# Attention probabilities and head outputs transposed by DMA instead of by TensorE, in a fused attention and mixture-of-experts kernel

## What is computed

```python
q = rms_norm((x @ wq).reshape(B, L, 16, 128), q_norm_w)
k = rms_norm((x @ wk).reshape(B, L, 4, 128), k_norm_w)          # then rope on q and k
k_ctx = rms_norm((ctx @ wk_ctx).reshape(B, T, 4, 128), k_norm_w)
scores = jnp.einsum('blhd,bmhd->bhlm', q, k_full) * scale + mask
probs = jax.nn.softmax(scores, axis=-1)
out = jnp.einsum('bhlm,bmhd->blhd', probs, v_full)
x = x + out.reshape(B, L, 16 * 128) @ wo
```

## Time and profile before

| | before |
|---|---|
| median of 3 runs | 376.57 us |
| the profiled execution's own run | 377.97 us |
| its span, first to last instruction | 376.3 us |
| PE busy | 343.7 us, 91% |
| VectorE busy | 325.6 us, 87% |
| ScalarE busy | 271.2 us, 72% |
| GpSimd busy | 165.8 us, 44% |
| mean granted clock of TensorE | 0.977 |
| moved by DMA | 13.49 MB |

### The profile page before, as it was taken

One profiled execution on the slowest core, in us unless ns is written; L12 is line 12 of the kernel. 1 busy time (PEld: TensorE's weight loads), 2 busy tenths in 40 slices (PEclk: granted clock), 3 DMA queues, 4 the chain that ended last, 5 costly groups with the idle time before them and its releaser, 6 DMA issues.

```text
span 376.3 us, 7781 instructions
## 1 busy us (share of the span) xinstructions
PE 343.7 (91%) x2471; PEld 237.3 (63%) x2476; DVE 325.6 (87%) x625; ACT 271.2 (72%) x913; POOL 165.8 (44%) x242
## 2 busy tenths in 40 slices
PE   6697798799999999999999999999999999998994
PEld 5373555376567665866685577567666778674572
DVE  1668999998999899899989998999899897759653
ACT  3557879676986797699759876986797567167562
POOL 3356565652754275427344443644174300334330
PEclk9788989999999999999999999999999999989999
DMA  5967000000030003000000000000000000000011
GB/s 179 379 212 223 17 0 2 1 2 14 3 111 0 14 0 111 14 1 0 0 14 0 0 0 14 0 0 0 0 0 1 2 0 2 2 0 3 22 35 57
DMA packets 11603, 13.49 MB, mean 36 GB/s; under 512 B 824, under 2 KB 9024, under 8 KB 11584
## 3 DMA queue, kind: packets, MB, share of 16 engines
q1 hardware_dynamic: 11584, 13.25, 11.0%
HBM read 12.20 MB, written 1.05 MB: 35 GB/s over the span
## 4 chain that ended last, share of the span: by engine, by line
PE 40%; DVE 24%; ACT 17%; issue 10%; POOL 4%; DMA 2%; SPq 1%; DVEq 1%; ACTq 0%; POOLq 0%
PE proj L1324 10%; ACT probs L524 8%; PE pt_ps L1300 5%; DVE probs L953 5%; PE proj L1157 4%; PE turn L1246 3%; DVE nmax L941 3%; DVE pT_lo L879 3%; PE o_ps L1310 3%; POOL q_rot L744 3%; PE sc_ps L1267 2%; ACT pT_hi L435 2%; DMA wq<-in_L_xattn_wq_dram 2%; ACT q_junk L468 2%; DVE q_t L870 2%
## 5 line engine op out<-in xcount | busy, mean ns | idle before, releaser
L524 ACT ACTIVATE probs<-sc_ps,nbias,q_r 128x256 f32<-128x256 f32 x128 | 70.8, 574 | 2.8 <-DVE nbias L945 2.8
L744 POOL TENSOR_TENSOR q_rot<-q_t 128x512 f32<-128x512 f32 x32 | 41.4, 1295 | 42.8 <-DVE q_t L872 42.0
L953 DVE TENSOR_SCALAR probs<-probs,rden 128x256 f32<-128x256 f32 x128 | 51.2, 461 | 1.1
L1157 PE MATMUL proj<-wq_hi,xT 128*128 128x512 f16 x128 | 40.1, 396 | 2.9 <-DVE wq_lo L863 2.9
L435 ACT ACTIVATE pT_hi<-pt_ps 128x512 f16<-128x512 f32 x64 | 34.8, 597 | 10.9 <-PE pt_ps L1300 10.9
L468 ACT ACTIVATE q_junk<-proj 128x128 bf16<-128x128 f32 x128 | 34.0, 295 | 11.7 <-DVE q_t L872 11.7
L879 DVE SCALAR_TENSOR_TENSOR pT_lo<-pt_ps,pT_hi 128x512 f16<-128x512 f32 x64 | 41.0, 682 | 0.6 <-ACT pT_hi L435 0.6
L941 DVE TENSOR_REDUCE nmax<-sc_ps 128x4 f32<-128x1024 f32 x32 | 38.9, 1214 | 1.5 <-PE sc_ps L1289 1.5
L831 POOL TENSOR_TENSOR wq<-xn_all,weight 128x512 bf16<-128x512 f32 x16 | 17.1, 1074 | 44.1 <-DVE weight L1098 23.4
L1324 PE MATMUL proj<-wo_hi,oT_hi 128*128 128x256 f16 x128 | 34.9, 273 | 0.0
L1324 PE MATMUL proj<-wo_lo,oT_hi 128*128 128x256 f16 x128 | 34.9, 273 | 0.0
(11 more groups left out here) (216 smaller groups left out, 920.7 us busy)
## 6 DMA issues: line engine op xcount, KB each, us to landing
wq<-in_L_xattn_wq_dram SPq DMA_DIRECT2D x4, 512.0 KB, 9.1
w<-in_L_ffn_w_dram SPq DMA_DIRECT2D x2, 1024.0 KB, 10.5
wq<-in_L_xattn_wo_dram SPq DMA_DIRECT2D x1, 2048.0 KB, 8.2
ctx_b<-in_ctx_dram SPq DMA_DIRECT2D x8, 128.0 KB, 2.1
out_dram<-x_all SPq DMA_DIRECT2D x4, 256.0 KB, 2.2
x_all<-in_x_dram SPq DMA_DIRECT2D x1, 896.0 KB, 12.3
wkc<-in_L_xattn_wk_ctx_dram SPq DMA_DIRECT2D x1, 512.0 KB, 4.2
wk<-in_L_xattn_wk_dram SPq DMA_DIRECT2D x1, 512.0 KB, 5.1
```

The source lines that it names most:

```text
L524: last = nc.scalar.activation(probs[:, h, :], sc_ps[:, h, :], ACT.Exp, bias=nbias[:, h:h + 1], scale=q_r[:, g, h:h + 1], accum_out=den[:, ...
L744: nc.gpsimd.tensor_tensor(q_rot[:], q_t1[:], q_t2[:], ALU.add).then_inc(q_added, 1)
L953: last = nc.vector.tensor_scalar(probs[:, h, :], probs[:, h, :], rden[:, h:h + 1], None, ALU.mult)
L1157: last = nc.tensor.matmul(bank[:], xT[:, a, c, :], w[:, c, cols], start=(n == 0), stop=(n == 3 * DC - 1))
```

## The change

The probabilities are no longer divided by their sum before the product with V, and TensorE no longer turns them. ScalarE rounds the undivided probabilities to f16 in SBUF (`p_round`, 128x1024), VectorE makes the rest (`p_rest`), and SyncE issues two transposing DMAs of 128x1024 f16 (256 KB each) into `pT_hi` and `pT_lo`, which have two slots. `p_hi` and `p_lo` have one slot: `p_round` and `p_rest` of a group wait until both DMAs of the group before have landed.

`mix` now has the turned probabilities as its stationary side and V as its moving side: per head 6 products of 128 columns, 24 in a group in place of 6 of 512. Its result has the tokens on the partitions. A group later VectorE multiplies it by the reciprocal sums (`o_scale`, 128x512 from PSUM), ScalarE rounds it (`o_round`), GpSimd makes the rest (`o_rest`), and two transposing DMAs of 128x512 f16 (128 KB each) bring `oT_hi` and `oT_lo`. `out_proj` is cut into four quarters (`out_part`), one in each group of the next row, summed in a bank of its own, `out_ps`; the residual and `second_norm` move to g=3.

Besides: `k_add` moves from VectorE to GpSimd. `kc` has a bank of its own (`kc_ps`) and stands after `k` and `q` on TensorE. On ScalarE `kc_copy` and `k_copy` stand after `p_round`, no longer between exponentials; `kc_scale` stands after `q_squares`. On GpSimd `kc_roots` stands after `q_add` and `k_roots`. wo is loaded in four pieces, w3 and w2 in four each. `xn2T` shares its memory with `w1_32`, and `ahead` and `tied` with `probs`. The sync engine's program is written out for all 32 groups. In the tail the order is adapted: quarters of `out_part` between the turns of weights, the router cut in two around `xn_copy(2)` and the last `o_scale`.

The core of the diff:

```diff
@@ sync
+            def turn_probs(b, g):
+                u = G * b + g
+                slot = u % 2
+                if u >= 2:
+                    sp.wait_ge(pv_done, u - 1)
+                for src, dst, split in ((p_hi, pT_hi, p_high), (p_lo, pT_lo, p_low)):
+                    sp.wait_ge(split, u + 1)
+                    sp.dma_start_transpose(dst[:, slot].rearrange("p h a t -> p (h a) t"),
+                                           src[:].rearrange("p h k -> p (h k)")).then_inc(d_pT[slot], 16)
+
+            def turn_out(b, g):
+                u = G * b + g
+                if b:
+                    sp.wait_ge(wo_part, u - G + 1)
+                for src, dst, split in ((o_hi, oT_hi, o_high), (o_lo, oT_lo, o_low)):
+                    sp.wait_ge(split, u + 1)
+                    sp.dma_start_transpose(dst[:, g, :].rearrange("p (h t) -> p h t", h=R),
+                                           src[:, g % 2, :]).then_inc(d_oT[g % 2], 16)
...
@@ scalar, row
-                    if g or not first:
-                        p_copy(u - 1)
-                    exps(b, g, (kc_copy, k_copy) if g == 3 and not last else ())
+                    exps(b, g)
                     if g == 1 and not first and not last:
                         ln_high(b + 1)
+                    p_round(b, g)
+                    if g == 3 and not last:
+                        kc_copy(b + 1)
+                        k_copy(b + 1)
+                    if g >= 2:
+                        o_round(b, g - 2)
+                    elif not first:
+                        o_round(b - 1, g + 2)
                     if g == 2 and not last:
+                        k_squares(b + 1)
                         kc_squares(b + 1)
                     if ahead_of(b, g, 2, last):
                         q_squares(*ahead_of(b, g, 2, last))
+                    if g == 2 and not last:
+                        kc_scale(b + 1)
...
@@ gpsimd, row
                     if g == 1 and not last:
                         ln_low(b + 1)
+                    if g == 3 and not last:
+                        q_roots(b + 1, 0)
+                    if g == 2 and not last:
+                        k_add(b + 1)
+                    if ahead_of(b, g, 2, last):
                         q_add(*ahead_of(b, g, 2, last))
                     if g == 2 and not last:
                         k_roots(b + 1)
+                        kc_roots(b + 1)
                         k_scale(b + 1)
+                    if g >= 2:
+                        o_rest(b, g - 2)
+                    elif not first:
+                        o_rest(b - 1, g + 2)
+                    if ahead_of(b, g, 2, last) and g != 2:
+                        q_roots(*ahead_of(b, g, 2, last))
+                    if g == 0 and not last:
+                        ln_root(b + 1)
+                    if g == 3 and not first:
+                        l2_root(b - 1)
...
@@ vector, row
-                    if g or not first:
-                        p_low(u - 1)
-                    if g == 2 and not first:
-                        second_norm(b - 1)
+                    if g >= 2:
+                        o_scale(b, g - 2)
+                    elif not first:
+                        o_scale(b - 1, g + 2)
+                    if g == 2 and not last:
+                        k_turn(b + 1)
...
-                    normalise(b, g)
+                    inv_den(b, g)
...
+                    p_rest(b, g)
+                    if g == 0:
+                        vc_low(b)
+                        v_low(b)
...
+                    if g == 3 and not last:
+                        kc_low(b + 1)
+                        k_low(b + 1)
...
+                    if g == 3 and not first:
+                        residual(b - 1)
+                        second_norm(b - 1)
...
@@ tensor
+            def mix(b, g):
+
+                u = G * b + g
+                seen(pe, o_scaled, u)
+                cols = slice(g * P, (g + 1) * P)
+                pe.wait_ge(*landed(d_pT, b, g))
                 for a in range(2):
                     for h in range(R):
+                        for i, (p, v) in enumerate(((pT_hi, v_hi), (pT_hi, v_lo), (pT_lo, v_hi))):
+                            last = nc.tensor.matmul(o_ps[:, h * P:(h + 1) * P], p[:, g % 2, h, a, :], v[:, a, cols],
...
@@ tensor, row
-                    if g or not first:
-                        turn_probs(b, g)
+                    if g == 2 and not last:
+                        k(b + 1)
...
                     if g == 1:
-                        if not first:
-                            out_proj(b - 1)
                         if not last:
                             turn_inputs(b + 1)
                         pe.wait_ge(vc_ready, b + 1)
...
+                    if not first:
+                        out_part(b - 1, g)
                     if g:
-                        mix(u - 1, g - 1)
+                        mix(b, g - 1)
```

353 lines of the change are left out of this document (175 added, 178 removed).

## The result

The changed kernel took 420.93 us, the median of 4 runs (419.65 to 421.62), against 376.86 for the kernel before (376.12 to 378.42, 4 runs): a ratio of 1.1159, 95% interval 1.1113 to 1.1205. The forecast was 400 with a range of 374 to 435. The sign, and the waits that make a steady row, came as foretold; the size was half of what happened, 23 us of 43, and the tail went otherwise than I had it.

The account below looks back on a forecast made before the run. TensorE, 91% busy, bounded the kernel before; afterwards waits between engines would: six rows of +3.2, clock 4, row 0 +3, last row -3.7, tail +0.5, 23 us more, for 400 us, range 374 to 435.

Parts of the forecast that it names:

- TensorE's lighter work is off the path: Steady rows: TensorE's work falls by 3.1 us to about 31, but waits between engines set the row.
- Stretch g=1: Scores of g=1 to scores of g=2: 9.7 us against 11.8, a gain of 2.1, with TensorE idle over 3 us.
- Stretch g=2 and 3: Scores of g=2 to the next row's g=0, longest chain through k: 18.0 us against 15.5, +2.5.
- the lock: VectorE's p_rest, reading two SBUF tensors, excludes GpSimd's q_add and o_rest, whichever starts first: 1.2 us a row.
- Stretch g=0: Scores of g=0 to scores of g=1, maximum held until 4.3 us by second_norm: 11.0 us against 8.2, +2.8.
- Clock: TensorE's steps on the chain, some 10 us a row, slow with the granted clock: 0.6 us a row, 4 in all.
- Rows 0 and 1: Row 0: +3 us (0 to +6), as g=1 gains nothing; row 1: as other steady rows, +3.2 besides the clock's 0.6.
- Tail: After the last scores: the last group's data chain reaches S+18.7, about level with before, +0.5 us for a slower DMA.
- DMA transposes: Transposing DMAs take 3 us (2.1 to 10.5) for probabilities, 2.5 in the tail's second step; up to about 5 adds nothing.
- TensorE as the bound: Rival: TensorE stays the bound, a row takes 32.5 us and the kernel 351; chance 0.10.
- Slow transposes: Rival: a 256 KB DMA beyond 6 us sets each group; at 7 us a group is 11.5, the kernel 455; chance 0.12.
- chain of waits: Main forecast: waits between engines make a row of 38.7 us, the kernel 400, own range 384 to 418; chance 0.74.

Follow-up runs that it names:

- turn_inputs_last: The changed kernel with turn_inputs moved behind out_part and mix in g=1 of every row: 401.34 us against 420.93.
- k_halves_first: The changed kernel with all order mends and, in g=3, kc_copy and k_copy ahead of p_round, kc_low and k_low ahead of p_rest: 367.07 us.
- kc_roots_first: The changed kernel with GpSimd's kc_roots ahead of k_roots in g=2: 415.66 us against 420.93.
- gap_kept_warm: The changed kernel with 48 unread products of 128 columns filling TensorE's idle ahead of turn_inputs in g=1: 413.99 us against 420.93.
- gpsimd_wo_behind_bias: The changed kernel with GpSimd's two long passes over wo each waiting for a VectorE bias: 416.58 us against 420.93.
- tail_mixed_early: The changed kernel with tail orders mended on three engines, including the last mix ahead of out_part 1 and out_part 3 ahead of shared_up: 410.97 us.

## Why the prediction was right, and where it fell short

- **TensorE's lighter work is off the path.** Right. TensorE is 80% busy (forecast near 80%) and leads 15% of the chain. `turn_inputs_last` to `k_halves_first` show that the lighter row is real, once the waits are gone: 33.7 against 35.5.
- **Stretch g=1, 9.7 us.** It took 11.5. The order and the idle of 3.09 us were right, and with the clock held up it is 9.9 (10.2 in rows 2 and 3). The step was also the dearest single one: moved back it gave 19.6 us. I had called this stretch a gain of 2.1, and it was one of 0.3; measured against what it could be (7.7 in `turn_inputs_last`) it is the main loss. A stretch that gets shorter can still hold the wait that makes the kernel slower.
- **Stretch g=2 and 3, 18.0.** 17.7, with each term in its place (q_rot 1.0 for the lock where I took 1.2). Shown by the timeline and by `kc_roots_first` and `k_halves_first`.
- **Stretch g=0, 11.0.** 11.1, and the maximum is 4.39 us after the scores. One detail was off: o_lo starts after ScalarE's o_hi at 270.71, which stands behind kc_copy and k_copy, and not only after p_rest; both ended within 0.1 us of each other.
- **Clock, 0.6 a row.** The mis-sized term of the rows. I scaled TensorE's steps by the mean clock of a busy share; but the 0.91 of the earlier trace rows is full clock with one piece of 3.4 us at half (48.2 to 51.7). So it is here: the clock halves for some 3.4 us right behind the idle, where `out_part` and `mix` are on the path: 1.6 to 1.7 us in a row in which it falls, shown by `gap_kept_warm`. Of the 23.3 us that rows 2 to 6 lost, that kernel gives back 6.4 (201.0 to 194.6), 1.3 a row, so these are the clock's and 16.9 the chain's, 3.4 a row where I had 3.2.
- **Rows 0 and 1.** For row 0 I had +3 and for row 1 what the other rows cost, 3.8; they are +1.9 and +7.9. I priced the lock for `p_rest` and had not looked at the bias, an operation of 0.16 us, beside GpSimd's passes over wo. In the kernel before it already took 2.18 us there, but I had read only a middle row. `gpsimd_wo_behind_bias` gives 4.4 us back in row 1.
- **Last row, -3.7.** -3.3. Here a transpose was not hidden, as I had it in every group: TensorE waits 1.14 us for pT_lo.
- **Tail, +0.5.** The largest miss: +15.0. I added up the chain of the data of the last group, S+18.7, as if its steps could start when their data are ready, and passed over what stands ahead of them on TensorE and ScalarE. The order was in the diff. I also put the clock of the tail at nothing, and half of its speed was granted for 20.5 us of it. And I counted from 306.3, while the last scores of the kernel before start at 305.6 (its last maximum is 2.4 us behind them, not 1.74), which moves the forecast by 0.7. `tail_mixed_early` gives 10.7 of the 15.0 back by a change of order alone, which also brought the clock back; the rest, 4.3 us, is not settled by a run; the path through two DMAs and a pass more, which I had thought level, is the likely place.
- **DMA transposes, 3 us and hidden.** 3.2 and 2.5. The Trainium skill ("DMA: Bandwidth & Descriptors", Latency and other measured facts) gives 261 GB/s, by which 128 KB more would take, as an estimate, 0.5 us; here they take 0.7 (3.2 against 2.5). The Trainium skill ("VectorE: DVE Perf Modes", The three transpose paths) gives 1309 ns for one block of 128x128; my estimate of eight such blocks in a row, 10.5 us, does not hold here: they land in 3.2.
- **The rivals.** TensorE as the bound, 351: no, and even with the orders mended the row is 33.7 and not 32.5. Slow transposes: no, and their formula held 2.2 us too much. The range was right by luck in part: 420.9 lies outside the 384 to 418 that I gave my own chain of waits, and inside 374 to 435 only because I had widened that for transposes of up to 6.3 us, which did not come.

In sum, of the 20 us that were missing: the tail came as 15.0 where I had 0.5; rows 2 to 6 as 23.3 where I had 19 (the chain 16.9 for 16, the clock 6.4 for 3); row 1, with some 4 of a lock that I had not priced there, as 7.9 for 3.8; row 0, the last row and the start together took 2 off.

## What to carry to other kernels

When an operation leaves an engine, look at what it was covering: `out_proj` and the order around it hid a wait of 3 us for the next row's inputs, and the wait plus the halved clock behind it cost nearly half of what the change lost. For a tail written out by hand, follow each engine's order with a clock in hand, not only the data; the sum along the data gives only a lower bound. And after such a change, mend the orders before judging it: the same operations took 421 us, 375 us and 367 us in three orders. Then look in the trace whether each mend did what it was for: one of the two waits on GpSimd did nothing, and the total alone did not show it.
